# Three low parts a chunk by adding DMAs instead of vector subtractions, in a three-layer field-interaction kernel

## What is computed

```python
x0 = xk = inputs                                   # (512, 39, 16)
for idx, (W, b) in enumerate(params):              # W (39, fields of xk, 128)
    z = relu(einsum('bhd,bkd,hks->bsd', x0, xk, W) + b[None, :, None])
    if idx != 2:
        xk = z[:, :64, :]
        direct.append(z[:, 64:, :])
    else:
        direct.append(z)
logit = sum(concatenate(direct, axis=1), axis=-1)  # (512, 256)
```

## Time and profile before

| | |
|---|---|
| median of 3 runs | 562.39 us |
| the profiled execution's own time | 562.33 us |
| its span | 560.5 us |
| TensorE busy (matmul) | 551.9 us, 98% |
| VectorE busy | 535.9 us, 96% |
| GpSimd busy | 499.5 us, 89% |
| ScalarE busy | 379.4 us, 68% |
| 16 DMA engines, main queue | 56.0% of the span |

### The profile page before, as it was taken

How to read it: one execution, slowest core, us unless ns; L and a number is a source line. 1 busy time by engine, 2 the same in 40 slices (tenths; PEclk the granted TensorE clock), 3 DMA queues, 4 the chain that set the end, 5 groups by cost and what they waited for, 6 DMA issues and landing times.

```text
span 560.5 us, 6190 instructions
## 1 busy us (share of the span) xinstructions
PE 551.9 (98%) x2008; PEld 374.9 (67%) x2008; DVE 535.9 (96%) x496; ACT 379.4 (68%) x427; POOL 499.5 (89%) x228
## 2 busy tenths in 40 slices
PE   7999999999999999999999999999999999999997
PEld 2435667667677677777767677677777767677665
DVE  4679999999999999999999999999999999999985
ACT  0436577776858767676776858777676876858662
POOL 0438899899999989999899999989999899999986
PEclk9999999999999999999999999999999999999999
DMA  8997391844828266391845828276391845826200
GB/s 326 418 408 317 132 370 34 325 191 181 344 87 331 108 254 271 146 361 30 331 183 183 342 95 333 98 262 263 150 363 29 333 177 192 333 99 215 81 1 20
DMA packets 21056, 122.17 MB, mean 218 GB/s; under 512 B 2720, under 2 KB 2976, under 8 KB 10784
## 3 DMA queue, kind: packets, MB, share of 16 engines
q1 hardware_dynamic: 20736, 121.51, 56.0%
q10 hardware_dynamic: 288, 0.26, 0.2%
HBM read 121.24 MB, written 0.52 MB: 217 GB/s over the span
## 4 chain that ended last, share of the span: by engine, by line
PE 82%; DVE 10%; issue 3%; ACT 2%; DMA 1%; POOL 1%; SPq 0%; DVEq 0%; POOLq 0%; ACTq 0%
PE z L611 82%; DVE raw L426 4%; DVE exact L426 3%; DVE d_raw L426 2%; DMA fields<-x_fields 1%; DVE lo L440 1%; POOL lo L515 1%; ACT hi L656 1%; ACT maps L675 0%; ACT final L696 0%; ACT L675 0%; DVE sums L453 0%; DVE sums L447 0%; SPq L358 0%; SPq L337 0%
## 5 line engine op out<-in xcount | busy, mean ns | idle before, releaser
L515 POOL TENSOR_TENSOR lo<-raw,hi 128x1024 fp32r<-128x1024 f32 x198 | 469.1, 2410 | 12.1 <-ACT hi L656 11.6
L656 ACT ACTIVATE hi<-raw 128x1024 fp32r<-128x1024 f32 (+1 forms) x213 | 219.1, 1029 | 125.1 <-DVE raw L426 112.0
L611 PE MATMUL z<-hi,w_hi 128*128 128x512 f32 (+1 forms) x559 | 220.8, 399 | 0.9 <-ACT hi L656 0.4
L426 DVE TENSOR_TENSOR raw<-spread,maps 128x1024 f32<-128x1024 f32 x184 | 219.0, 1210 | 2.1 <-ACT maps L675 2.1
L611 PE MATMUL z<-hi,w_lo 128*128 128x512 f32 x513 | 202.5, 395 | 0.0
L611 PE MATMUL z<-lo,w_hi 128*128 128x512 f32 x544 | 196.7, 451 | 0.2 <-POOL lo L515 0.2
L611 PE MATMUL z<-exact,w_exact 128*128 128x512 f32 (+1 forms) x386 | 180.4, 594 | 2.8 <-DVE exact L426 2.0
L611 PEld LDWEIGHTS z<-lo,w_hi 128*128 128x128 f32 x544 | 101.2, 188 | 56.2 <-issue 31.5
L611 PEld LDWEIGHTS z<-hi,w_hi 128*128 128x128 f32 (+1 forms) x559 | 104.8, 188 | 31.4 <-ACT final L696 3.7
L611 PEld LDWEIGHTS z<-exact,w_exact 128*128 128x128 f32 (+1 forms) x386 | 72.1, 189 | 68.0 <-issue 53.7
L611 PEld LDWEIGHTS z<-hi,w_lo 128*128 128x128 f32 x513 | 96.2, 188 | 22.9 <-issue 0.5
(11 more groups left out here) (21 smaller groups left out, 69.6 us busy)
## 6 DMA issues: line engine op xcount, KB each, us to landing
spread<-x_spread SPq DMA_DIRECT2D x80, 1024.0 KB, 8.1
fields<-x_fields SPq DMA_DIRECT2D x31, 768.0 KB, 6.8
fields<-x_fields SPq DMA_DIRECT2D x15, 512.0 KB, 5.6
w_exact<-w SPq DMA_DIRECT2D x10, 256.0 KB, 14.7
spread<-x_fields SPq DMA_DIRECT2D x1, 768.0 KB, 10.1
raw<-w SPq DMA_DIRECT2D x1, 640.0 KB, 6.7
spread<-x_fields SPq DMA_DIRECT2D x1, 512.0 KB, 10.7
out<-sums SPq DMA_DIRECT2D x2, 240.0 KB, 4.2
```

The source lines that it names most:

```text
L426: nc.vector.tensor_tensor(products, by_field, by[0:rows, :].unsqueeze(1).to_broadcast([rows, tiles, COLS]), ALU.mult).then_inc(ready, 1)
L515: nc.gpsimd.tensor_tensor(low_part(layer, c, k), raw[low_rows(layer, k), PLACE[S][layer, c, k] % RAW_RING, 0:tiles_in(layer, k), :], hi[lo ...
L611: mm = nc.tensor.matmul(z_of(layer, c)[:, :], w[0:rows, :], part[0:rows, :], start=(step == FIRST_STEP[layer, c] and p == 0), stop=(step = ...
L656: nc.scalar.activation(hi[0:rows, count % HI_RING, 0:tiles, :], products, ACT.Copy).then_inc(hi_ready, 1)
```

## The change

It adds a fourth kind, **A**. The product of an A couple is written by VectorE to one of two fixed places in SBUF that lie over the fp32 weights of tiles 0 to 7 of layers 1 and 2 (free after the first chunk, since there those couples are no longer E). ScalarE writes the high part and then, as a second activation, the negated high rounding of the product (scale -1) into a place of `added`, of two couples. GpSimd waits for it and issues a DMA that adds the product to it in place (`accum_op=ALU.add`), 512 KB of fp32. TensorE takes the result as the low part, `A_LAG` = 5 couples after the high part. The kinds, rings, lags and positions change too. GpSimd's work gets an order of its own (`POOL_ORDER`): an A step stands one couple after its product. `SPREAD_RING` is 7 in both kernels.

```diff
-KINDS = ("SDES", "ESDSESSDSS", "SSDSSESDES")
-KINDS_FIRST = ("EEEE", "ESEEEEEEEE", "EESEEESEES")
+KINDS = ("SEES", "SDASASDSES", "ADSSESESDS")
+KINDS_FIRST = ("EEEE", "EEEEEEESEE", "EESEEEEESS")
...
-LO_LAGS = (2, 1, 1)
+LO_LAGS = (1, 1, 1)
+
+ADD_LAG = 1
+A_LAG = 5
 D_LAG = 3
 
-EXACT_RING = 4
-RAW_RING = 6
-HI_RING = 5
-LO_RING = 4
+EXACT_RING = 3
+RAW_RING = 3
+HI_RING = 8
+LO_RING = 3
...
-SUM_LAST_AT = 6
-SUM_DIRECT_AT = 6
-COPY_AT = 2
-FINISH_AT = 2
+SUM_LAST_AT = 5
+SUM_DIRECT_AT = 4
+COPY_AT = 1
+FINISH_AT = 3
 MAPS1_AT = 5
-MAPS2_AT = 3
-
-
-
-KEPT = 7
+MAPS2_AT = 2
+
+
+
+KEPT = 6
...
+POOL_ORDER = sorted((couple for couple in LOW if couple in PLACE["SA"]),
+                    key=lambda couple: (AT[couple] + ADD_LAG if couple in PLACE[A] else
+                                        max(AT[c] for c in LOW[:USED[couple] + 1] if c in PLACE[S])
+                                        + LO_LAGS[couple[0]]))
...
+        a_raw = [w_exact[n][:, 0:A_RAW_TILES, :].rearrange("p t s -> p (t s)").rearrange("p (t c) -> p t c", c=COLS)
+                 for n in (1, 2)]
+        added = sb("added", [128, 2, 2, COLS], fp32r)
...
+                    elif kind == A:
+                        if count >= 2:
+                            wait_added(dve, COUPLE[A][count - 2])
+                        else:
+                            wait_weights_done(1 + count)
+                        products, ready = a_raw[count % 2], a_raw_ready
...
+            def add_low(layer, c, k):
+                place = PLACE[A][layer, c, k]
+                pool.wait_ge(negated_ready, place + 1)
+                if place >= 2:
+                    wait_added(pool, COUPLE[A][place - 2])
+                nc.gpsimd.dma_start(low_part(layer, c, k),
+                                    a_raw[place % 2],
+                                    accum_op=ALU.add).then_inc(a_lo_ready[place % 2], 16)
...
+                    if kind == A:
+                        if PLACE[A][layer, c, k] >= 2:
+                            act.wait_ge(lo_used, USED[COUPLE[A][PLACE[A][layer, c, k] - 2]] + 1)
+                        nc.scalar.activation(low_part(layer, c, k), products, ACT.Copy,
+                                             scale=-1.0).then_inc(negated_ready, 1)
```

More of the change, by code:

```diff
@@ L50, in tiles_of @@
     return [t for t in range(LAYER_TILES[layer]) if any(kinds(layer, c)[t // 2] in wanted for c in (0, 1, 2))]
-SPLIT_TILES = [tiles_of(n, S + D) for n in range(3)]
+SPLIT_TILES = [tiles_of(n, S + D + A) for n in range(3)]
 assert SPLIT_TILES[0][:-1] == list(range(len(SPLIT_TILES[0]) - 1)) and SPLIT_TILES[0][-1] == TILES0 - 1
 assert KINDS[0][-1] != E and KINDS_FIRST[0] == E * COUPLES[0]
-assert all(KINDS[n][-1] != E for n in (1, 2))
-LO_LAGS = (2, 1, 1)
+assert all(KINDS[n][-1] not in E + A for n in (1, 2)) and A not in KINDS[0]
+LO_LAGS = (1, 1, 1)
+ADD_LAG = 1
+A_LAG = 5
 D_LAG = 3
-EXACT_RING = 4
-RAW_RING = 6
-HI_RING = 5
-LO_RING = 4
+EXACT_RING = 3
+RAW_RING = 3
+HI_RING = 8
+LO_RING = 3
 QUADS = TILES // 4
@@ L70 @@
 WEIGHT_CUTS = (0, 4, 8, 12, 16, TILES)
+A_RAW_TILES = 2 * COLS // OUT
+assert all(E not in KINDS[n][:A_RAW_TILES // 2] and A not in KINDS_FIRST[n] for n in (1, 2))
 WEIGHTS_AHEAD = 1
 WARM = 3
-SUM_LAST_AT = 6
-SUM_DIRECT_AT = 6
-COPY_AT = 2
-FINISH_AT = 2
+SUM_LAST_AT = 5
+SUM_DIRECT_AT = 4
+COPY_AT = 1
+FINISH_AT = 3
 MAPS1_AT = 5
-MAPS2_AT = 3
-KEPT = 7
+MAPS2_AT = 2
+KEPT = 6
 LAST = CHUNKS - 1
@@ L166 @@
 USED = {couple: n for n, couple in enumerate(LOW)}
-S_LOW = {couple: n for n, couple in enumerate(c for c in LOW if c in PLACE[S])}
-assert len(USED) == len(PLACE["SD"])
+LOW_OWN = [couple for couple in LOW if couple not in PLACE[A]]
+LOW_PLACE = {couple: n for n, couple in enumerate(LOW_OWN)}
+AT = {}
+for _layer, _c, _couples in SEGMENTS:
+    for _k in _couples:
+        AT[_layer, _c, _k] = len(AT)
+POOL_ORDER = sorted((couple for couple in LOW if couple in PLACE["SA"]),
+                    key=lambda couple: (AT[couple] + ADD_LAG if couple in PLACE[A] else
+                                        max(AT[c] for c in LOW[:USED[couple] + 1] if c in PLACE[S])
+                                        + LO_LAGS[couple[0]]))
+S_LOW = {couple: n for n, couple in enumerate(c for c in POOL_ORDER if c in PLACE[S])}
+assert len(USED) == len(PLACE["SDA"])
 def pair_places():
@@ L283, in wait_multiplied, with wait_added @@
             kind = kinds(layer, c)[k]
-            engine.wait_ge({E: exact_ready, S: raw_ready, D: d_raw_ready}[kind], PLACE[kind][layer, c, k] + 1)
+            if kind == E:
+                engine.wait_ge(exact_ready, PLACE[E][layer, c, k] + 1)
+            elif kind == D:
+                engine.wait_ge(d_raw_ready, PLACE[D][layer, c, k] + 1)
+            elif kind == S:
+                engine.wait_ge(raw_ready, PLACE[S][layer, c, k] + 1)
+            else:
+                engine.wait_ge(a_raw_ready, PLACE[A][layer, c, k] + 1)
+        def wait_added(engine, couple):
+            place = PLACE[A][couple]
+            engine.wait_ge(a_lo_ready[place % 2], 16 * (place // 2 + 1))
         def wait_contracted(engine, layer, c):
@@ L315, in low_part @@
             if rest(layer, k):
-                return hi[low_rows(layer, k), PLACE["SD"][layer, c, k] % HI_RING, 0:1, :]
-            return lo[:, USED[layer, c, k] % LO_RING, :, :]
+                return hi[low_rows(layer, k), PLACE["SDA"][layer, c, k] % HI_RING, 0:1, :]
+            if kinds(layer, c)[k] == A:
+                return added[:, PLACE[A][layer, c, k] % 2, :, :]
+            return lo[:, LOW_PLACE[layer, c, k] % LO_RING, :, :]
         def z_of(layer, c):
@@ L433, in multiply, with wait_weights_done @@
                         split_lo(layer, c, k)
+            def wait_weights_done(n):
+                dve.wait_ge(weights_lo[n], sum(a < A_RAW_TILES for _, a, _ in RUNS[n]))
+                for k in range(A_RAW_TILES // 2):
+                    if kinds(n, 0)[k] == E:
+                        dve.wait_ge(exact_used, PLACE[E][n, 0, k] + 1)
             def split_lo(layer, c, k):
-                count = USED[layer, c, k]
-                place = PLACE["SD"][layer, c, k]
+                count = LOW_PLACE[layer, c, k]
+                place = PLACE["SDA"][layer, c, k]
                 dve.wait_ge(hi_ready, place + 1)
@@ L540, in weights0_split_lo @@
                                         ALU.subtract).then_inc(weights_lo[0], 1)
-            for layer, c, k in LOW:
-                if kinds(layer, c)[k] != S:
-                    continue
+            def add_low(layer, c, k):
[6 more added lines that the diff above has]
+                                    accum_op=ALU.add).then_inc(a_lo_ready[place % 2], 16)
+            for layer, c, k in POOL_ORDER:
                 if (layer, c) == (1, 0):
@@ L554, in _ @@
                     weights_split_lo(2, TILES)
-                split_lo(layer, c, k)
+                if kinds(layer, c)[k] == S:
+                    split_lo(layer, c, k)
+                else:
+                    add_low(layer, c, k)
         @block.tensor
@@ L571, in contract @@
                     else:
-                        count = PLACE["SD"][layer, c, k]
+                        count = PLACE["SDA"][layer, c, k]
                         if what == "hi":
@@ L576, in contract @@
                             pe.wait_ge(s_lo_ready, S_LOW[layer, c, k] + 1)
+                        elif kind == A:
+                            wait_added(pe, (layer, c, k))
                         else:
@@ L588, in contract @@
                                 pe.wait_ge(weights_last_lo[layer], 1)
-                    high, low = hi[:, count % HI_RING, :, :], lo[:, USED.get((layer, c, k), 0) % LO_RING, :, :]
+                    high = hi[:, count % HI_RING, :, :]
+                    low = None if kind == E else low_part(layer, c, k)
                     passes = []
```

21 lines of the change are left out of this document (14 added, 7 removed).

## The result

The changed kernel takes 568.59 us (median of 4 runs, 567.74 to 569.6) against 562.41 before: ratio 1.0107, 95% interval 1.0095 to 1.012. It is 6.2 us slower, where 2.1 us faster was forecast. Every ratio here compares fast executions alone, which leaves out one of 2994 us of the sixth run's kernel. The profiled execution took 567.74 us, its span is 565.9.

What follows compares the result with a forecast made beforehand. The prediction took TensorE's list, 33.5 us a chunk, to bound the kernel. Its terms -0.3, -1.1, -0.5 and -0.2 summed to -2.1 us, giving 560.3 us, in a range from 559.0 to 580.

Steps and rivals of the forecast that it cites:

- What bounds the kernel: Whole kernel: TensorE's list sets the pace at 33.5 us a chunk, with VectorE and GpSimd within 1.5 us of it.
- VectorE and GpSimd: Each chunk: VectorE falls from 33.4 to 32.3 us, GpSimd to 30.5 us, both under TensorE's 33.5.
- GpSimd's issue: Each of three adding DMAs a chunk: issuing takes GpSimd 1.07 us, free up to 2.07 us; effect 0.
- the rival that GpSimd becomes the bound: Each chunk: above 2.07 us an issue GpSimd's list exceeds TensorE's; at 2.41, +1.0 us a chunk, 578 us; chance 0.12.
- The adding DMA, at 0: Layer 1's couple 4, called tightest: landing of 8.1 us hidden by about 9 us of cover, so 0.
- The rival: End of layer 1, every chunk: landing over 9 us makes TensorE wait; +30 us at 11, +85 at 14.7; chance 0.18.
- The wait for `final`, -1.1 us: Start of layer 2: VectorE further ahead removes TensorE's 0.08 us wait a chunk, -1.1 us over some 14 chunks.
- the bound of 0 that was named for FINISH_AT 3: Start of layer 2: 0 gained if one more high part and a negation ahead of `final` keep the wait as long.
- The ends: First layer 1: S couple moved from place 1 to 7, -0.5 us; last layer 2: cover for maps2, -0.2 us (-1 to +1).
- The tight rings at 0: Change from layer 2 to 1: VectorE's lead absorbs GpSimd's missing 2.2 us, 0; as a rival +2 to +8 us, chance 0.08.
- The list, -0.3: First chunks: 6 more fp32r passes and 2 fewer fp32 matmuls on TensorE, -0.3 us.

Runs made afterwards that it cites:

- sixth run: The kernel before, with VectorE's last layer 2 weight subtraction and its three ScalarE weight roundings moved ahead of layer 1 of chunk 1: 565.35 us, ratio 1.0045.
- fifth run: The changed kernel with VectorE's last layer 2 weight subtraction moved ahead of layer 1 of chunk 1, and A_LAG 6 in place of 5: 561.23 us, ratio 0.9974.
- eleventh run: The fifth run's kernel with FINISH_AT 2 in place of 3: 562.09 us, ratio 0.9993.
- seventh run: The changed kernel with the early weight subtraction, SyncE holding loads until layer 2's adding DMA has landed, then spread first, fields last: 671.66 us, ratio 1.1939.
- second: The changed kernel with A_LAG 6 in place of 5, nothing else: 565.95 us, ratio 1.0059.
- third: The changed kernel loading one field tile of each load instead of up to three from chunk 2 on: 573.28 us, ratio 1.0183.
- ninth run: The fifth run's kernel with layer 0's second couple made D (one exact couple less), its low lag 2, HI_RING 8: 610.48 us, ratio 1.085.

## Why the prediction was wrong

**What bounds the kernel: right.** TensorE's list at 0.233 and 0.427 us holds where the granted clock is 1.0, and once the two losses are off, TensorE alone is the chain for 497 us.

**VectorE and GpSimd: right in kind.** GpSimd's issue was put at 1.07 us and took 0.81; the rival that GpSimd becomes the bound is out.

**The adding DMA, at 0: wrong by the landing.** This is the first step that failed, and it turned the steady run's -1.1 us into +2.0. I took 8.1 us for all landings and costed one place, couple 4 of layer 1. Its cover came out as said: issue 296.89, used at 306.42, 9.5 us. But from chunk 2 on the two A couples of layer 1 land in 4.5 to 6.4 us, at a time when less is loaded: the DMA engines moved 228 and 148 GB/s while the two from 293.5 on were under way, and 349 GB/s during that of layer 2. The A couple of layer 2 was not costed at all. It is issued (first row) while the three field loads of 277.5 us and the first `spread` load of 279.8 are under way, and two more `spread` loads follow at 282.0 and 286.6; the second row is its use:

```profile
281.59 0.59 POOL L599 DMA_DIRECT2D added<-w_exact  x1
...
292.22 0.74 PE L676 MATMUL z<-added,w_hi 128*128 128x512 f32 x2
```

It landed 10.59 us after its issue and was used at once, at 10.63. TensorE would have used it some 10.5 us after the issue, and from chunk 2 on the landings in layer 2 took 9.5 to 11.4 us, but for the last chunk, which has no loads to make: 5.1 us. The earlier trace rows showed the idle window, and the same row shows the burst; the step that I left out was to put all three DMAs of a chunk on it. That alone would not have been enough: at 8.1 us the couple of layer 2 would have passed as covered too. The price was wrong as well, 8.1 us for what takes 4.5 to 6.4 in one place and 9.5 to 11.4 in the other. The rival named the mechanism (a landing over its cover, every chunk) with the wrong couple and price: 2.0 us in the run and 0.8 in chunk 1, not 30, because the landing misses the cover by under 1 us, and on the chain after 90 us in only 3 chunks.

**The wait for `final`, -1.1 us: mis-sized.** With the landing out of the way, in the fifth run, TensorE still stands 0.8 us in the steady run, where it stood 1.1 before. So this term was worth 0.3 us: its weight loads wait for `final` in 12 chunks, 5.6 us in all, and the term came out nearer to the bound of 0 that was named for FINISH_AT 3. The eleventh run, with FINISH_AT 2, comes down to 0.4.

**The transition, costed at nothing: wrong, and the larger part.** The sum had no term for chunk 1. VectorE's subtraction on weights had taken 1.83 us for 64x128 elements, where the row sum on 128x512 takes 0.67; that row was the warning, and I read past it. It was 1.83 because it got its turn when the running GpSimd subtraction ended. In the changed kernel, with two adding DMAs and weight runs of other sizes, GpSimd was busy from 55.27 to 65.32 without a break, and the turn came only at the end. Moving it away from GpSimd's work gave back 4.2 of the 6.2 us. Whoever costs a moved or denser GpSimd list must count the VectorE instructions with both operands in SBUF beside it. The Trainium skill, SBUF — State Buffer, section on who interferes with whom, states this: a VectorE instruction with two SBUF inputs contends with a GpSimd instruction that reads SBUF. The traces agree: 5.64 us beside GpSimd's subtractions, 0.29 for the same instruction with GpSimd idle. The prediction weighed that section only for writing DMA descriptors.

**The ends: right in sign, the last layer 2 undersized and for another reason.** -0.5 at the first layer 1 measured -0.6, up to the end of layer 2's head of chunk 0. The last layer 2, put at -0.2 for the longer cover of `maps2`, gave -1.4. The eleventh run has the same tail and loses the 1.4 us again, so it is FINISH_AT 3 that saves them; the prediction counted that move only as a possible cost.

**The tight rings at 0: right in this kernel, for a reason not seen.** Alone they cost 35 us on the kernel before. Here GpSimd is idle for some 5 us in 35 (busy 30.1 us from 276 to 311, 33.5 before); that this room is what pays for them is argued, not shown. With A_LAG 6 a high ring of 7 costs 37 us.

The forecast of 560.3 us is close to what the two repairs give, 561.23, but that is in part luck. The list, -0.3, was right. Of the others, the fifth run's trace has 0.3 us of the 1.1 for `final`, 1.4 us in the last layer 2 where 0.2 was forecast, and 1.2 us more in the second stretch, which the sum didn't have. The first stretch, forecast at -0.5, is 0.3 longer in that trace, where the granted clock was 0.50 for 3.4 us from 8.0 us on, which it was not in the trace before.

## What to carry to other kernels

Where one engine's list sets the pace, relief elsewhere is worth little, and what a new asynchronous step can break decides the sign: put every instance of it on the timeline of what shares its resource, not the tightest by buffer order alone. An instruction that takes several times what its size says may already be in conflict in the kernel before; find its opponent before making that opponent busier. Ring sizes, lags and the relief of an engine are one edit here, and a price for one of them alone does not hold. And the position of one small instruction in an in-order engine can be a gain at one end of the kernel and a loss in its middle: `final` one couple later costs 0.4 us in the run and saves 1.4 in the last layer 2.

## What the runs showed of the hardware

- A 512 KB SBUF-to-SBUF adding DMA issued by GpSimd landed in 4.2 to 5.6 us with the loads held back (seventh run) and in 9.4 to 12.0 beside the 1 MB loads (layer 2 in the changed kernel and in the second, third and fifth runs); the page's median hides both groups.
- It cost GpSimd 0.59 to 1.25 us of issue, 0.81 in the mean, a third of the subtraction that it replaces.
- A VectorE subtraction of 64x128 elements with both inputs in SBUF took 0.29 to 5.64 us, by what GpSimd did meanwhile. In the kernel before and in the sixth run it ended 0.15 us after the GpSimd subtraction that it had met. In the changed kernel it didn't get in at the first boundary. There, right behind two DMA issues, GpSimd's records stand 0.65 us into each other (subtractions of 3.0 us that start 2.37 apart; 2.4 us each and 0.05 of overlap before). That this is why is not shown.
- VectorE's tensor_tensor instructions with one input in PSUM kept their 1.21 us beside a busy GpSimd.
- After TensorE had stood 2.15 us at a start of layer 2, the granted clock was 0.50 for 3.4 us (ninth run).
- Fewer bytes ahead of a DMA need not make it earlier: with the field loads cut from 2 to 0.75 MB a chunk, layer 2's adding DMA landed after 11.0 us in the median instead of 10.5.
